# Two kinds of VectorE instructions of a graph-and-expert kernel issued in two halves each

## The reference

```python
x = x + gnn0(layernorm(x))   # segment_sum(edge_weight * (n @ weight_l)[src], dst) + n @ weight_r + biases
x = x + ffn0(layernorm(x))   # 8 experts, each relu(bn(.)) twice, output sum weighted by a softmax gate
x = x + gnn1(layernorm(x))   # segment_sum(edge_weight * (n @ weight)[src], dst) + bias
x = x + ffn1(layernorm(x))   # 32 experts, the one with the largest logit of each node
```

## Time and profile before

| | us |
|---|---|
| median of 3 runs | 3136.0 (3130.68 to 3143.77) |
| the profiled execution, its own time | 3133.19 |
| its span, first to last instruction | 3131.3 |
| second stage, about | 411 to 1795 |

### The profile page before, as it was taken

How to read it: one execution, slowest core, us unless ns; L and a number is a source line. 1 busy time by engine, 2 the same in 40 slices (tenths; PEclk the granted TensorE clock), 3 DMA queues, 4 the chain that set the end, 5 groups by cost and what they waited for, 6 DMA issues and landing times. The chain is left out here.

```text
span 3131.3 us, 54480 instructions
## 1 busy us (share of the span) xinstructions
PE 2684.4 (86%) x19092; PEld 2474.8 (79%) x19092; DVE 2161.1 (69%) x5110; ACT 1557.7 (50%) x3295; POOL 1971.0 (63%) x1696
## 2 busy tenths in 40 slices
PE   5899826899999999999999737888888989888889
PEld 5788725798888888888888626788888888888889
DVE  8888654588787878778876565665666666666663
ACT  3477555788888888888886410111111111111112
POOL 0455467678888888888880076666666666666660
PEclk9999957899999999999999967899998999899999
DMA  2143453233333332333231176767776776767760
GB/s 70 6 94 77 101 156 105 82 93 110 93 101 109 108 111 83 110 108 112 86 110 35 36 226 172 183 172 179 179 178 172 179 175 176 181 176 179 178 171 13
DMA packets 241962, 390.31 MB, mean 125 GB/s; under 512 B 43642, under 2 KB 115218, under 8 KB 241426
## 3 DMA queue, kind: packets, MB, share of 16 engines
q0 software_dynamic: 163072, 310.24, 38.6%
q1 hardware_dynamic: 78324, 74.90, 7.7%
q10 hardware_dynamic: 288, 1.61, 0.1%
HBM read 343.43 MB, written 43.19 MB: 123 GB/s over the span
## 5 line engine op out<-in xcount | busy, mean ns | idle before, releaser
L1408 POOL DMA_INDIRECT f_got<-h_tab,list_cols x784 | 991.5, 1265 | 251.4 <-issue 221.3
L2120 POOL DMA_INDIRECT n_got<-h_tab,edge_cols x784 | 807.9, 1031 | 427.9 <-issue 220.5
L2184 ACT ACTIVATE n_hrh<-bank 128x512 fp32r<-128x512 f32 x196 | 117.0, 597 | 644.3 <-DMA list<-runs,off_i 355.0
L1689 DVE TENSOR_TENSOR f_hlo<-edge_cols,f_hhi 128x1024 fp32r<-128x1024 f32 (+1 forms) x208 | 241.9, 1163 | 259.6 <-ACT f_hhi L1497 189.1
L2394 DVE SCALAR_TENSOR_TENSOR n_hrl<-bank,n_hrh 128x512 fp32r<-128x512 f32 x196 | 135.1, 689 | 379.6 <-ACT n_hrh L2184 305.8
L1467 ACT ACTIVATE f_got<-f_got,list_cols 128x256 f32<-128x256 f32 x784 | 333.4, 496 | 116.3 <-DMA f_got<-h_tab,list_cols 110.9
L1584 PE MATMUL bank<-f_mhi,f_hot 128*128 128x256 f32 x1168 | 307.3, 296 | 56.9 <-DVE f_mlo L1683 50.6
L1492 ACT ACTIVATE edge_cols<-bank,f_shf,f_scl 128x512 f32<-128x512 f32 (+1 forms) x416 | 292.1, 743 | 94.4 <-PE bank L1399 39.7
L2231 PE MATMUL bank<-n_got,n_hot_h 128*128 128x256 f32 x784 | 244.0, 311 | 79.9 <-DMA n_got<-h_tab,edge_cols 36.7
L1585 PE MATMUL bank<-f_mlo,f_hot 128*128 128x256 f32 x1168 | 305.4, 295 | 3.5 <-issue 3.5
L400 POOL DMA_INDIRECT list<-runs,off_i x98 | 159.9, 1631 | 217.5 <-DVE off_i L759 100.4
(11 more groups left out here) (329 smaller groups left out, 7882.4 us busy)
## 6 DMA issues: line engine op xcount, KB each, us to landing
f_got<-h_tab,list_cols POOLq DMA_INDIRECT x784
n_got<-h_tab,edge_cols POOLq DMA_INDIRECT x784
n_rows<-acc_tab SPq DMA_DIRECT2D x24, 256.0 KB
out_rows<-n_rows SPq DMA_DIRECT2D x24, 256.0 KB
h_tab<-acc SPq DMA_DIRECT2D x37, 128.0 KB
edge_cols<-in_w SPq DMA_DIRECT2D x16, 256.0 KB
acc<-in_x SPq DMA_DIRECT2D x4, 896.0 KB
h_tab<-hbuf SPq DMA_DIRECT2D x7, 512.0 KB
```

The lines of the kernel that those rows point to most:

```text
L1408: nc.gpsimd.indirect_dma_start(got[:, s % RING0, u, :], None, h_tab[0], bass.IndirectOffsetOnAxis(gidx0[:, s * U + u:s * U + u + 1], 0), b ...
L1689: nc.vector.tensor_tensor(hlo[l][:, :, 0:w], rl[:, :, 0:w], hhi[l][:, :, 0:w].bitcast(F32), ALU.subtract).then_inc(s_lo[l], 1)
L2120: nc.gpsimd.indirect_dma_start(got[:, s % RING, u, :], None, h_tab[1], bass.IndirectOffsetOnAxis(gidx[:, s * U + u:s * U + u + 1], 0), bou ...
```

## The change

The one-hot table and the lower parts of the messages are each made by two DVE instructions, which cover two of the slot's four edge tiles, in place of one that covers four. The semaphore is raised by the second. Waits, order, buffers and values stay. `lower_half` is as before, one instruction.

```diff
-                    nc.vector.tensor_tensor(hot[:, s % 2, :, 0:n], iota_f[:, 0:n].unsqueeze(1).broadcast_to([P, U, n]),
-                                            rel_f[:, s * U:s * U + U].unsqueeze(2).broadcast_to([P, U, n]),
-                                            ALU.is_equal).then_inc(s_hot, 1)
+                    for at in (0, U // 2):
+                        c = s * U + at
+                        last = nc.vector.tensor_tensor(hot[:, s % 2, at:at + U // 2, 0:n],
+                                                       iota_f[:, 0:n].unsqueeze(1).broadcast_to([P, U // 2, n]),
+                                                       rel_f[:, c:c + U // 2].unsqueeze(2).broadcast_to([P, U // 2, n]),
+                                                       ALU.is_equal)
+                    last.then_inc(s_hot, 1)
...
-                    nc.vector.tensor_tensor(mlo[:, s % 2, :, :], got[:, s % RING0, :, :],
-                                            mhi[:, s % 2, :, :].bitcast(F32), ALU.subtract).then_inc(s_mlo, 1)
+                    for part_of in (slice(0, U // 2), slice(U // 2, U)):
+                        last = nc.vector.tensor_tensor(mlo[:, s % 2, part_of, :], got[:, s % RING0, part_of, :],
+                                                       mhi[:, s % 2, part_of, :].bitcast(F32), ALU.subtract)
+                    last.then_inc(s_mlo, 1)
```

## The result

The changed kernel takes **3243.3 us** (median of 4 runs, 3232.7 to 3251.5) where the kernel before takes 3135.2 us (4 runs, 3130.7 to 3143.8) on the same chip: ratio 1.0325, 95% interval 1.0292 to 1.0359. The forecast was 3115, its range 3088 to 3143. The profiled execution took 3236.9 us, 103.7 more than the one before. In the changed kernel the halves of the one-hot table are L1679 and those of the lower parts L1688, `lower_half` is L1695 and `add_out` L1712; POOL's and ACT's lines are the old ones.

What follows compares the result with a forecast made beforehand. The prediction took POOL's gather issue to bound the second stage. 25 us from shorter groups plus 4 in the start-up less 9 of DVE cost gave 20 us off 3136, rounded to 3115 us, range 3088 to 3143.

Steps and rivals of the forecast that it cites:

- POOL paces the stage: Second stage: POOL's issue rate of gathers sets the pace in most slots, 6.35 us a slot, 101.7 us a group.
- A gather is held by a DVE instruction with two SBUF operands and let in at the seam: Second stage: gathers get in between halves; of 162 us of stalls some 93 stay, mean gather 1285 to about 1170 ns.
- An instruction more costs 0.07 to 0.15 us on DVE: Second stage: fixed part of each of 392 added DVE instructions, 27 us in all, at most 58 us.
- What of it shows is 1 us a group: Second stage: part of the added DVE time that delays PE's waits for `hlo`, 9 us over nine groups.
- 4 us in the start-up: Gain before 637 us, where POOL does little but edges: 4 us, between 0 and 6.
- What paces the stage when POOL doesn't: Second stage: with POOL off the path, groups fall from 101.8 to 99.0 us, 25 us won over nine.
- more is won: Rival: without late gathers, second-stage groups come down towards PE's 95.25 us; 56 us won, 3080 us; chance 0.09.
- The rivals: Alternatives to the forecast: gain given back (3132 to 3140 us, 0.25), more won (3080, 0.09), slower (3148 to 3163, 0.11).
- Slower: Rival: second-stage gathers are not let in between halves, while DVE's instructions grow; 3148 to 3163 us; chance 0.11.

Runs made afterwards that it cites:

- f2: Changed kernel with two idle memsets a slot on POOL before the second stage's gathers; 3219.6 us, 1.0107 of the kernel before, chip IV.
- e3: Changed kernel with three idle memsets a slot on POOL before the second stage's gathers; 3034.6 us, 1.0398 of the kernel before, chip II.
- e1: Kernel before with only the one-hot table in halves; 2908.1 us, 0.9954 of the kernel before, chip II.
- e2: Kernel before with only the lower parts of the messages in halves; 2906.4 us, 0.9949 of the kernel before, chip II.
- e4: Kernel before without every fourth gather from the second stage's fifth slot on; 2845.4 us, 0.9744 of the kernel before, chip II.
- f1: Kernel before without every fourth gather from the second stage's fifth slot on; 3072.1 us, 0.9651 of the kernel before, chip IV.
- h2: Changed kernel with second-stage gathers of half the width from the fifth slot on; 2881.6 us, 0.9864 of the kernel before, chip VI.
- g3: Changed kernel without every fourth gather from the second stage's fifth slot on; 3083.0 us, 0.9679 of the kernel before, chip V.
- h1: Changed kernel without every fourth gather in second and third stages, third block scaled again in the second; 2781.4 us, 0.9539 of the kernel before, chip VI.
- e5: Changed kernel run again unaltered; 3244.6 us, 1.0320 of the kernel before, chip III.
- e6: Kernel before run again for its profile; 3126.9 us in one run, chip III.
- g4: Kernel before with both instructions whole but over the first half of their data alone; 3279.7 us, 1.0294 of the kernel before, chip V.
- f3: Changed kernel with one idle memset a slot on POOL before the second stage's gathers; 3235.9 us, 1.0159 of the kernel before, chip IV.
- g1: Kernel before with only the one-hot table in halves; 3237.4 us, 1.0149 of the kernel before, chip V.
- g2: Kernel before with only the lower parts of the messages in halves; 3228.1 us, 1.0110 of the kernel before, chip V.
- e8: Changed kernel with PE waiting on its own earlier completions, at most about 50 entries ahead; 3244.7 us, 1.0327 of the kernel before, chip III.
- f4: Changed kernel without the second stage's matmuls of the messages' lower part; 3216.5 us, 1.0093 of the kernel before, chip IV.

## Why the prediction was wrong, point by point

- **POOL paces the stage: right.** Idle work on POOL lengthens the slot and makes ACT wait for gathers (115 us in f2, 134 in e3, against 58 before), each part of the change alone shortens it on chip II (e1, e2), and with a gather less POOL waits for `f_mlo` and the slot falls to 6.05 us (e4, f1).
- **A gather is held by a DVE instruction with two SBUF operands and let in at the seam: right, but that the size came out to 1 ns is luck.** Forecast mean 1170 ns, measured 1171, and 1189 in h2. The forecast took the holds of the two instructions one by one, and they depend on each other, since a gather let in sooner meets another DVE instruction. I put each hold down to the instruction under way when the gather starts, from 700 to 1650 us: before, `f_mlo` 75 us, `f_hlo` 50, `f_hot` 28 (the prediction counted to the instruction that let the gather in, and had 88, 37 and 28). In e2, on II, with `f_mlo` alone in halves, `f_mlo` falls to 39, but `f_hot` rises to 46, so that the mean fell by 30 ns and not by the 85 that 51 us in 598 gathers stand for. In the changed kernel they are 6, 50 and 20 us in 540 gathers. The Trainium skill ("SBUF — State Buffer", "Who interferes with whom") infers that a `tensor_tensor` does not stall descriptor generation; the runs say otherwise, as a gather ends 0.89 us after such an instruction, and as the gathers got 114 ns shorter where only the length of such instructions was changed.
- **An instruction more costs 0.07 to 0.15 us on DVE: right.** DVE is busy 84.5 us a group instead of 82.0: 2.5 us for 32 instructions more, 0.08 each.
- **What of it shows is 1 us a group: right.** With POOL off the path the kernel before takes 6.053 us a slot (e4 on II, f1 on IV) and the changed one 6.098 (g3 on V, h1 on VI): 0.7 us a group, the same to the third digit on chips of both kinds.
- **4 us in the start-up: not decided.** The first pair has 4.5 us; the same two kernels on chip III differ by 15 (199.5 us in e5, 214.7 in e6).
- **"What paces the stage when POOL doesn't", 101.8 to 99.0, 2.8 us a group won: this step failed.** On chip I a group went to 112.8 us. The 25 us of gain became 99 us of loss in nine groups, and 13.4 more in the third. The step took for granted that, once POOL is ahead, PE's, ACT's and DVE's own times set the pace, and drew that pace from one group in which POOL had a lead. On chips I, III, IV and V a third thing comes in when gathers are let through faster: TensorE's completions are late, by 5 to 7 us in the stretch shown, about twice a group. On chip VI, where they aren't, h2's nine groups from 718.0 to 1599.5 us take 97.9 us each. Against chip I's 101.8 that is 3.9 us won and not 2.8; the kernel before wasn't profiled on VI. In all h2 wins 39 us, 1.4%, where 20 us had been forecast, between the forecast and the rival "more is won". So there the one group's 99.0 was somewhat high; e4 puts the floor at 96.8.
- **The rivals:** none was it. "Slower" was there for gathers that are not let in. They were let in, and the time was lost elsewhere, in waits that no rival names.

What is shown: the loss is in the groups in which completions are late (168 us of waits on them where there were 6; in the stretch shown the new waits of PE, DVE and POOL stand behind them); they come with gathers let through, in whole instructions too (g4), and go when gathers are left out with the change in place (g3) or held up by idle work on POOL (f2). What separates the kernels on such chips is narrow: the kernel before, at 4 gathers in 6.33 to 6.36 us, has 6 to 10 us of late waits on I and III. With one memset a slot (f3), where POOL could keep 6.11 us, it is 133 us, and g1 and g2, the kernels that ran at 6.26 us on II, have 133 and 108 on V. On I and III the kernel before stands just below the edge.

What stays open: the cause behind it, and with it why TensorE is late at all. It is not how far PE's list runs ahead, to the bound that e8 sets, and not the number of matmuls alone (f1, f4). Nor is it how long PE goes without a pause over 0.1 us: in f1 that is 85 us with nothing late, in g4, which has the most late waits, 28 us at most, in f2 38. Nor does the trace show the blocks of instructions slow to arrive: of their 16 KB transfers from 700 to 1650 us the longest took 1.46 us in the changed kernel and 1.63 in the kernel before. Whether it is the number of gathers, their bytes, or how many go unheld in a row was not measured on a chip that shows it. In f1 and g3 the fourth block of rows fades towards zero, since ACT scales it in place every time; h1, which keeps it alive, ran on chip VI, so a part of TensorE's operands in it isn't excluded there. f2, with nothing left out, stands without that doubt. Nor was the whole change with full gathers run on a chip of the other kind. That the kernel before loses some time the same way on IV and V is likely, though it wasn't profiled there: removing a gather gains 111 us on IV (f1) and 75 on II (e4). And the third stage is 1362 to 1367 us long in f1 to f4 and 1356 to 1360 in g1 to g4; taken off the kernel before's 3183 and 3187 us, it leaves a second stage that ends at some 1817 and 1827 us, against 1792 on I. That is an estimate of 25 to 35 us lost, and it would put the kernel before past the edge on these two.

No version here that does all the work beats the kernel before on both kinds of chip: the whole change loses 3% on I and III and each part 1 to 1.5% on V, and the parts win 0.5% on II.

## What to carry to other kernels

When the engine that paces a stage is relieved, the new pace needs a measurement of its own; a single stretch of the old trace in which that engine happened to be ahead gave 99.0 us, where h2 had 97.9 and the changed kernel 112.8. A slow issuer can also be what keeps a stage below an edge beyond which something else stalls: look for waits that the profile puts down to nothing, in the kernel before too ("remote", 6 us here, and far more in its third stage), as they tell what lies close by. And a gain of half a per cent should be measured on more than one chip, with the old kernel beside it each time.

## What the runs showed of the hardware that had not been expected

- The same kernel takes 2921 us on two chips and 3135 to 3187 on the others. Most of the difference is in the third stage, which the change leaves alone: 5.3 us a slot in h2 on VI and e1 on II, 6.35 in the first profile of the kernel before and 6.43 in g3 on V. From 2000 to 2900 us, first g1 on V, then h2 on VI: 5716 and 6955 matmuls, at a clock of 0.91 and 1.00.

```profile
2000.00:2900.00 900.00, 792.71 (x5716) 755.47 (x5716) 544.99 (x1941) 143.09 (x379) 567.09 (x556) 0.91 0.70 173
```

```profile
2000.00:2900.00 900.00, 856.88 (x6955) 834.13 (x6954) 631.24 (x2198) 175.37 (x452) 623.04 (x613) 1.00 0.76 192
```

- In that stage too, on chips I, III, IV and V, ACT has long waits that the profile puts down to nothing, often some 25 us apart; in e1, e3, h1 and h2, on II and VI, there is none. In the kernel before, from 2000 to 2900 us:

```profile
ACT list_cols L2177 <- remote: 138.3, 15, 10.5
```

- While completions are late, the starts that the trace shows can go on for dozens of matmuls, or come in groups some 1.43 us apart (1041.45, 1042.89, 1044.29, 1045.73 and 1047.16 us in the changed kernel). The granted clock is full up to 1044.45 us and falls then, in the midst of these groups. From 700 to 1650 us it falls 17 times, 13 of them for 6.8 us.
